# Context matmuls of an attention step in two halves of 256 columns, with the score matmuls in pairs between them and the maximum units apart

## The reference

```python
mod = (silu(c) @ wmod).reshape(4, 6, 1, 128); sa, ca, ga, sb, cb, gb = ...   # ga, gb: sign kept, size at least 0.25
h = layernorm(x) * (1 + ca) + sa
q, k, v = (h @ Wq.T, h @ Wk.T, h @ Wv.T), 16 heads of 8; q, k = rotary(q), rotary(k)
attn = softmax(q @ k.T / sqrt(8));  x = x + ga * ((attn @ v) @ Wo.T)
h = layernorm(x) * (1 + cb) + sb
logits = silu(h @ rw1 + rb1) @ rw2 + rb2;  w = softmax over the top 2
x = x + gb * (h + sum_e w_e * (silu(h @ we1_e + be1_e) @ we2_e + be2_e))
```

## Time and profile before

| what | value |
|---|---|
| median of three executions | 1004.0 us |
| profiled execution, its own time | 1003.83 us |
| its span, first to last instruction | 1002.0 us |
| busy share PE, DVE, ACT, POOL | 87%, 78%, 74%, 35% |
| `prepare` and the first 16 + 16 units, to the first C | 0 to 117 us |
| the 256 steps, first C to the last one | 117 to 802 us |
| last turned context and `mix` | 802 to 1002 us |

### The profile page before, as it was taken

The page is one execution under the profiler, slowest core; times in us unless marked ns, Lnnn a source line. Parts: engine busy times, 40 slices in busy tenths (PEclk is TensorE's granted clock), DMA queues, the critical chain, the costliest instruction groups (busy, mean ns, idle before and its releaser), DMA issues. The chain is left out here.

```text
span 1002.0 us, 17987 instructions
## 1 busy us (share of the span) xinstructions
PE 871.9 (87%) x5950; PEld 352.4 (35%) x5950; DVE 783.9 (78%) x1058; ACT 742.3 (74%) x1636; POOL 347.0 (35%) x649
## 2 busy tenths in 40 slices
PE   6554799999999899899989989998998859998991
PEld 3330122222222222222222222231222159998991
DVE  5959899999998988999898899989886117643386
ACT  5550488888888888888888888888887846666661
POOL 5522000000002452161235226133522616477573
PEclk9775599999999999999999999999999979999996
DMA  5671032240330000071000001100000112223553
GB/s 139 239 282 75 1 144 74 107 172 33 145 123 31 25 33 2 33 226 41 10 25 33 1 33 38 40 13 22 1 1 2 44 41 59 59 65 83 134 149 93
DMA packets 60378, 71.80 MB, mean 72 GB/s; under 512 B 9949, under 2 KB 42212, under 8 KB 60288
## 3 DMA queue, kind: packets, MB, share of 16 engines
q1 hardware_dynamic: 55456, 61.82, 18.9%
q0 software_dynamic: 4544, 8.44, 2.6%
q10 hardware_dynamic: 288, 0.40, 0.1%
HBM read 30.08 MB, written 41.06 MB: 71 GB/s over the span
## 5 line engine op out<-in xcount | busy, mean ns | idle before, releaser
L895 DVE TENSOR_REDUCE half_max<-ps_max 128x2 f32<-128x1024 f32 x512 | 601.8, 1218 | 64.9 <-PE ps_max L711 60.3
L826 ACT ACTIVATE probs<-ps_scores 128x512 f32<-128x512 f32 x1024 | 540.2, 604 | 93.6 <-PE ps_scores L732 91.9
L745 PE MATMUL ps_ctx<-probs,v_grp 128*32 128x512 f32 x2048 | 273.7, 606 | 0.7 <-ACT probs L826 0.7
L732 PE MATMUL ps_scores<-q_set,k_set 51*128 51x512 bf16 x1024 | 261.0, 387 | 12.9 <-ACT probs L826 8.6
L711 PE MATMUL ps_max<-k_set,q_set 48*128 48x512 bf16 x1024 | 187.9, 395 | 48.1 <-DVE half_max L895 34.7
L732 PEld LDWEIGHTS ps_scores<-q_set,k_set 51*128 51x128 bf16 x1024 | 68.8, 93 | 324.5 <-ACT probs L826 296.6
L1534 ACT ACTIVATE hid<-ps_up,w_tile 128x128 f32<-128x128 f32 x312 | 88.9, 367 | 48.1 <-PE ps_up L1701 47.9
L638 POOL CAST max_parts<-row_max 128x16 bf16<-128x16 f32 x32 | 6.3, 196 | 307.8 <-DVE row_max L903 307.4
L1502 POOL DMA_INDIRECT y_rows<-y,slots_in x78 | 89.9, 1152 | 65.8 <-DVE y L1571 50.1
L711 PEld LDWEIGHTS ps_max<-k_set,q_set 48*128 48x128 bf16 x1024 | 50.4, 95 | 147.0 <-DVE half_max L895 131.3
L1701 PE MATMUL ps_up<-slots_t,w_tile 128*128 128x128 f32 x624 | 84.6, 280 | 2.3 <-DVE w_tile L1565 2.3
(11 more groups left out here) (200 smaller groups left out, 624.1 us busy)
## 6 DMA issues: line engine op xcount, KB each, us to landing
slots<-zero_rows SPq DMA_DIRECT2D x43, 387.0 KB, 4.9
q_terms<-parts SPq DMA_DIRECT2D x24, 256.0 KB, 2.8
k_terms<-parts SPq DMA_DIRECT2D x24, 256.0 KB, 3.2
q_set<-q_terms SPq DMA_DIRECT2D x32, 192.0 KB
k_set<-k_terms SPq DMA_DIRECT2D x32, 192.0 KB
slots_in<-slots SPq DMA_DIRECT2D x78, 64.5 KB, 1.9
rows<-y_rows SPq DMA_DIRECT2D x16, 256.0 KB, 4.9
q_set<-max_rows SPq DMA_DIRECT2D x128, 3.0 KB
```

The lines of the kernel that those rows point to most:

```text
L732: pe.matmul(bank[:], k_set[g % SETS][operand, u, tile * P:(tile + 1) * P], q_set[g % SETS][operand, u, c * BANK:(c + 1) * BANK], start=Tru ...
L745: ins = pe.matmul(ps_ctx[32 * head:32 * head + 32, :], v_grp[g % 2][:, tile, head, :], probs[:, s % RING, head, :], start=tile == 0, stop= ...
L826: act.activation(probs[:, s % RING, place, :], ps_scores[n % BANKS_S][:], ACT.Exp, scale=float(HD) ** -0.5).then_inc(slot_taken, 1)
L895: dve.reduce_max(half_max[tile // HT % 2][:, c, 2 * u:2 * u + 2, tile % HT], ps_max[n % 2][:].rearrange("p (r n) -> p r n", r=2), axis=AX. ...
```

## The change

C of a step becomes two halves of 256 query columns each. Only the first half of the first key tile carries the start flag, which clears the bank's marks; only the second half of the last tile carries the stop flag. The waits stand at the first half, `ctx_added` counts at the second. The order on PE becomes: first half of C, S2 and S3 of step s+1, second half of C, first maximum unit, S0 and S1 of step s+2, second maximum unit, what stands beside. The slot order, ACT's order and the lead-in follow: one more score tile (place 1) is made a step ahead, and the copy of `ps_ctx` stands after exp 2 and before exp 3, as before.

```diff
-    order = [("negated", 0)] + [(0, place) for place in range(GH)] + [(1, 0)]
+    order = [("negated", 0)] + [(0, place) for place in range(GH)] + [(1, 0), (1, 1)]
     for s in range(ALL_STEPS):
         if s + 1 < ALL_STEPS:
-            order += [(s + 1, place) for place in range(1, GH)]
+            order += [(s + 1, 2), (s + 1, 3)]
         if s + 2 < ALL_STEPS:
-            order.append((s + 2, 0))
+            order += [(s + 2, 0), (s + 2, 1)]
         order += beside(s)
...
-            def add_ctx(s):
+            def add_ctx(s, half):
                 g, tile = s // STEPS, s % NT
-                pe.wait_ge(slot_taken, SLOT[s, GH - 1] + 1)
...
+                columns = slice(half * BANK // 2, (half + 1) * BANK // 2)
+                if half == 0:
+                    pe.wait_ge(slot_taken, SLOT[s, GH - 1] + 1)
...
                 for head in range(GH):
-                    ins = pe.matmul(ps_ctx[32 * head:32 * head + 32, :], v_grp[g % 2][:, tile, head, :],
-                                    probs[:, s % RING, head, :], start=tile == 0, stop=tile == NT - 1)
+                    ins = pe.matmul(ps_ctx[32 * head:32 * head + 32, columns], v_grp[g % 2][:, tile, head, :],
+                                    probs[:, s % RING, head, columns],
+                                    start=tile == 0 and half == 0, stop=tile == NT - 1 and half == 1)
...
-                ins.then_inc(ctx_added, 1)
+                if half == 1:
+                    ins.then_inc(ctx_added, 1)
...
                 first, second = units(s)
+                add_ctx(s, 0)
                 if s + 1 < ALL_STEPS:
-                    scores(s + 1, 1)
                     scores(s + 1, 2)
-                add_ctx(s)
-                if s + 1 < ALL_STEPS:
                     scores(s + 1, 3)
+                add_ctx(s, 1)
+                if first is not None:
+                    max_scores(first)
                 if s + 2 < ALL_STEPS:
                     scores(s + 2, 0)
+                    scores(s + 2, 1)
                 if first is not None:
-                    max_scores(first)
                     max_scores(second)
...
             def step(s):      # ScalarE
                 if s + 1 < ALL_STEPS:
-                    exp(s + 1, 1)
                     exp(s + 1, 2)
                 if s % NT == NT - 1:
                     copy_ctx(s // NT)
...
                     exp(s + 1, 3)
                 if s + 2 < ALL_STEPS:
                     exp(s + 2, 0)
+                    exp(s + 2, 1)
```

More of the change, by code:

```diff
@@ L734, in scores @@
                           start=True, stop=True).then_inc(slot_ready, 1)
-            def add_ctx(s):
+            def add_ctx(s, half):
                 g, tile = s // STEPS, s % NT
-                pe.wait_ge(slot_taken, SLOT[s, GH - 1] + 1)
[L740 to L743, removed]
+                columns = slice(half * BANK // 2, (half + 1) * BANK // 2)
+                if half == 0:
+                    pe.wait_ge(slot_taken, SLOT[s, GH - 1] + 1)
+                    if s % STEPS == 0:
+                        pe.wait_ge(v_ready, g + 1)
+                    if tile == 0 and s:
+                        pe.wait_ge(ctx_t_ready, s // NT)
                 for head in range(GH):
-                    ins = pe.matmul(ps_ctx[32 * head:32 * head + 32, :], v_grp[g % 2][:, tile, head, :],
-                                    probs[:, s % RING, head, :], start=tile == 0, stop=tile == NT - 1)
-                    if head == 0 and s % STEPS == STEPS - 1:
+                    ins = pe.matmul(ps_ctx[32 * head:32 * head + 32, columns], v_grp[g % 2][:, tile, head, :],
+                                    probs[:, s % RING, head, columns],
+                                    start=tile == 0 and half == 0, stop=tile == NT - 1 and half == 1)
+                    if half == 0 and head == 0 and s % STEPS == STEPS - 1:
                         ins.then_inc(set_used, 1)
-                    if head == 0 and s % STEPS == 0 and s:
+                    if half == 0 and head == 0 and s % STEPS == 0 and s:
                         ins.then_inc(v_used, 1)
-                ins.then_inc(ctx_added, 1)
+                if half == 1:
+                    ins.then_inc(ctx_added, 1)
             def turn_negated(h):
@@ L812, in _ @@
             scores(1, 0)
+            scores(1, 1)
             for s in range(ALL_STEPS):
@@ L885, in _ @@
             exp(1, 0)
+            exp(1, 1)
             for s in range(ALL_STEPS):
```

## The result

The changed kernel takes 992.27 us (median of four executions, 989.75 to 994.53) against 1003.63 of the kernel before beside it: ratio 0.988, 95% interval 0.985 to 0.991. On another chip it took 991.43, ratio 0.989 (0.987 to 0.990). The profiled execution is one of 991.75 with a span of 989.9.

A forecast was written before the change was run, and what follows sets the result against it. Bound before: C in a row with one exp, 2.40 us a step; after, DVE's ring, 2.30. Sum: 1003.83 - 15.0 + 3.3 + 2.4 + 1.0 - 3.8 = 991.7, said 992; own range 986 to 997.

The forecast's parts named there:

- The old ring: Plain step before the change: C in a row with one exp, 2.40 us worked out against 2.39 in the trace.
- PE's 2.01 of before: PE's own work in a plain step of the kernel before, 2.01 us, leaving 0.38 to spare.
- A half C, 0.57, and PE's 2.24: On PE, half a C takes 0.57 us; PE's work per step rises by 0.23 to 2.24.
- rival of dearer halves: Halves of C or shape changes beside them cost more on PE: 1004, or 1014 with exposed weight load; chance 0.20.
- Rings through exp: Half C, S2 and S3, exp 2, exp 3: 2.14 us a step; S1 has 0.04 of room.
- fourth rival: Scores S2 and S3, or S0 and S1, don't run side by side: 998 to 1006 us; chance 0.05.
- The ring through DVE, 2.30: Second maximum unit waits for DVE's reduction two before it: 4.60 us for two steps, the longest ring of the change.
- Groups of eight: Eight steps with their interruptions: 19.80 us against 20.30, saving 0.50, or 15.0 in 30 groups with maximum units.
- Routing: Steps beside routing give back gain: 3.3 us for pieces on PE, 2.4 for DVE, 1.0 for POOL waits.
- third rival: Gain given back through S1's room, pieces, exp behind the copy and POOL: 1000 to 1003 us; chance 0.13.
- The last steps: From step 240, without maximum units: 2.14 us a step instead of 2.39, 15 x 0.25 = 3.8 saved.
- DVE as the only bound: Steps take DVE's own 2.26 us: 982, or 979 if turned maxima hide; range 977 to 985, chance 0.17.

The follow-up runs named there:

- units late: Changed kernel with both maximum units together behind the second pair of scores (S0 and S1 of step s+2): 1018.93 us, ratio 1.015 to the kernel before.
- lighter DVE: Changed kernel with each reduction over 256 instead of 512 columns of a unit, which changes the output: 952.03 us.
- even units: Changed kernel with the first maximum unit moved ahead of C's second half, units 1.11 us apart instead of 0.45: 984.82 us, ratio 0.982.
- later copy: ACT's context copy moved behind exp 3: 979.16 us on the kernel with the first maximum unit ahead of C's second half, 991.29 on the changed kernel alone.

## Why the prediction was right

The forecast was 992, measured 992.27; its parts hold as follows.

- *The old ring.* Shown in part: with DVE at half its work the old steps do not move, and PE's own work was not the limit either, since the changed kernel gives it more to do and takes less time. That the 2.40 is C in a row with one exp is what the intervals add up to; exp was not made shorter by itself.
- *PE's 2.01 of before.* The list names four steps of 0.23 and would add up to 2.24. The order has three (scores to unit, unit to unit, unit to scores), and 2.01 is the right sum.
- *A half C, 0.57, and PE's 2.24.* Measured 0.57 in every place and 2.22 where nothing waits. The reason given was wrong in a piece that did not reach the sum: I put 0.05 of fixed cost on each C, and the split alone showed it to be nothing. The 0.14 goes with the change of the array's shape, which each half in the new order has on both sides and adjacent halves have not. The data type changes at the same places, from bf16 to fp32 and back; but the transpose of the maxima is bf16 in another shape and takes the same 0.32 behind a unit (333.49 to 333.81). The rival of dearer halves is out. Of the Trainium skill's rule of the drain ("TensorEngine Tiling (Array Packing)", "Key Properties") the trace agrees that a change of mode costs, with 0.32 instead of 0.22 ahead of C and 0.14 behind it. The new kind, unit to C, costs the 0.32 of the kinds that were there; no further 0.07 came.
- *Rings through exp.* The room of 0.04 for S1 was real: no pair starts apart in plain steps, so the fourth rival is out, and where the room was taken away (units late), S1 came 0.18 late. The last steps take 2.13 (769.88 to 772.01 below), against 2.14 worked out:

```profile
769.88 0.64 PE L747 MATMUL ps_ctx<-probs,v_grp 128*32 128x256 f32 x8
...
772.01 0.64 PE L747 MATMUL ps_ctx<-probs,v_grp 128*32 128x256 f32 x8
```

- *The ring through DVE, 2.30.* Measured 2.31, over two quiet steps. It is shown from both sides: lighter DVE and even units each take it away, units together lengthen it.
- *Groups of eight.* 19.80 worked out, 19.72 measured (118.30 / 6), against 20.30. The single steps agree too when they are counted as the prediction counts them, from second unit to second unit (202.43 to 222.15, from behind one turned context to behind the next): 2.39, 2.37, 2.53, 2.40, 2.26, 2.37, 2.59 and, with the turned context, 2.81. Worked out in the same order were 2.38, 2.43, 2.59, 2.38, 2.28, 2.32, 2.61 and 2.81.
- *Routing.* In steps 64 to 239 I had 22 x 0.50 - 6.7 = 4.3 of gain, measured 4.9. The two parts are both off: a group gains 0.58 and not 0.50 (3.5 / 6), which makes 12.8 of 22 groups, so that routing takes back about 8 and not 6.7. In that measure the third rival was partly right. None of the three losses that I put on routing (pieces, DVE, POOL) was tested by itself.
- *The last steps.* 3.8 worked out, 3.1 measured. The plain step falls as forecast, 15 x 0.26 = 3.9. But what the two turned contexts and the copies add was 37.7 - 15 x 2.39 = 1.85 before and is 34.6 - 15 x 2.13 = 2.65 now; I had put nothing on that.
- *The beginning and the end.* In the first two groups 1.0 was forecast and 0.2 measured in this execution, whose clock rose later. From exp 3 of step 0 to exp 3 of step 16 the kernel before takes 41.7, and the changed one 40.6 in the profile with the earlier clock. Behind the steps 0.4 came that nobody had worked out.
- *Luck in the sum.* The parts are off by +0.5, +0.6, -0.7, -0.8 and +0.4. That they add up to 12.1, the forecast, is luck. That each is under 1 us is not: the ring and the groups of eight carry most of the gain, and they came out as worked out.
- *DVE as the only bound*, the second rival, is what the changed kernel could have been: even units and the later copy give 979.16, and the rival's figure was 979. It did not happen in the change because the units stand 0.45 apart (even units alone give 6.6 us) and because C waits for exp 3 behind the copy (about 5.7 more, once the units are even).

## What to carry to other kernels

When all engines look full, write down the rings of dependence between them with the starts from the timeline, one price for each edge; here that gave 2.40 for 2.39 and then 2.30 for 2.31. An engine that looks busy without a gap can still be in such a ring with another one. Cutting the long operation of such a ring and putting other work between its pieces pays although it adds work; the pieces should be placed so that each of the other rings gets its waiting time filled, here 1.08 us for a bank and 1.13 for a reduction. A visible wait is worth its length only if nothing else would be waited for at nearly the same time: list all that the waiting instruction needs. The later copy took away the wait for exp 3 and left the wait for the copy, which gave nothing in one order and about 0.6% in the other.

## What was unexpected

- Two fp32 products of 256 columns take the same 1.00 us as one of 512 when they follow each other in the same shape (ratio of the kernels 1.002, 0.999 to 1.005).
- Even units and the later copy with a full DVE reach the same 38.60 us for 16 steps as the changed kernel with DVE at 57% of its busy time (21.3 of 37.5).
- The order of the change with a whole C is 5.2% slower than the kernel before, the split alone is no faster, and both together are 1.2% faster: neither part has a gain of its own.
- Two executions of one kernel differ by 1.5 us at step 16, and TensorE's clock rose to 2.4 GHz later in the slower one (0.70 against 0.84 from 115 to 130 us). That is more than the gain of 16 steps of this change.
